# Even lag product ahead of the eight matches: two operations of an attention loop change places on VectorE and on TensorE

## What is computed

```python
qf, kf = fft(q, axis=2), fft(k, axis=2)                 # over the 64 tokens of a sequence
corr = ifft(qf * conj(kf), axis=2).real                 # correlation at 64 lags
w, idx = top_k(corr.transpose(0, 1, 3, 2), 8)           # the 8 best lags of each feature
w = softmax(w, axis=-1)
out = sum(w[i] * take(v, min(idx[i] + pos, 63)) for i in range(8))
x = x + out                                             # then x = x + moe(layernorm(x))
```

## Time and profile before

| | us |
|---|---|
| Median of 3 runs | 490.2 (487.67 to 490.48) |
| Profiled execution, whole time | 490.35 |
| Profiled execution, span of the core | 488.5 |
| Busy in the span: PE / DVE / ACT / POOL | 449.0 / 309.7 / 265.4 / 278.1 |
| Attention loop, from the first correlation maxima (pass 0) to those of pass 15 | 15.37 to 179.94 |
| One steady pass | 11.07 |

### The profile page before, as it was taken

The page is one execution under the profiler, slowest core; times in us unless marked ns, Lnnn a source line. Parts: engine busy times, 40 slices in busy tenths (PEclk is TensorE's granted clock), DMA queues, the critical chain, the costliest instruction groups (busy, mean ns, idle before and its releaser), DMA issues.

```text
span 488.5 us, 8388 instructions
## 1 busy us (share of the span) xinstructions
PE 449.0 (92%) x2272; PEld 334.6 (68%) x2272; DVE 309.7 (63%) x943; ACT 265.4 (54%) x521; POOL 278.1 (57%) x331
## 2 busy tenths in 40 slices
PE   3589999999999999958999998998999999999997
PEld 1456666655666664523368897897888999888885
DVE  2789899999999985488422647542333444248873
ACT  3868888888888873641102346554555665322120
POOL 2346667667666644494777287777656600077730
PEclk9989999999999999979999999998999999999999
DMA  4516733444443222211996568686888654268952
GB/s 160 194 43 235 283 130 129 150 165 160 162 144 130 86 88 86 84 46 57 316 388 251 208 221 304 239 303 223 290 261 291 204 198 152 108 176 259 320 194 86
DMA packets 40012, 91.89 MB, mean 188 GB/s; under 512 B 5024, under 2 KB 5024, under 8 KB 39712
## 3 DMA queue, kind: packets, MB, share of 16 engines
q1 hardware_dynamic: 32544, 62.00, 35.9%
q0 software_dynamic: 7424, 29.37, 17.8%
HBM read 49.92 MB, written 41.42 MB: 187 GB/s over the span
## 4 chain that ended last, share of the span: by engine, by line
PE 53%; DVE 16%; DMA 10%; issue 7%; POOL 7%; ACT 5%; SPq 1%; DVEq 0%; POOLq 0%; ACTq 0%
PE bank L471 36%; DMA x2T<-x_slots 7%; PE bank L656 4%; PE bank L572 3%; DVE top_v L955 3%; POOL arena L1215 3%; POOL arena L1218 3%; PE bank L483 3%; PE bank L581 3%; DMA resid<-x 2%; DVE stats L918 2%; DVE arena L960 2%; DVE resid L943 2%; ACT arena L787 1%; ACT arena L786 1%
## 5 line engine op out<-in xcount | busy, mean ns | idle before, releaser
L471 PE MATMUL bank<-ring,xgT_hi 128*128 x376 | 70.4, 285 | 0.0
L471 PEld LDWEIGHTS bank<-ring,xgT_hi 128*128 128x128 f32 x376 | 62.2, 193 | 4.0
L471 PE MATMUL bank<-ring,xgT_lo 128*128 x188 | 53.6, 285 | 0.0
L1103 DVE TENSOR_TENSOR xgT_lo<-bank,xgT_hi 128x512 fp32r<-128x512 f32 x47 | 32.3, 690 | 31.1 <-ACT xgT_hi L839 26.7
L1255 POOL TENSOR_TENSOR ring<-x2T,ring 128x1536 fp32r<-128x1536 f32 x14 | 49.3, 3520 | 1.2
L1303 POOL DMA_INDIRECT x2T<-y_rows,pos_i x16 | 16.2, 1014 | 43.1 <-DMA y_rows<-xg_sb 38.5
L1126 DVE TENSOR_TENSOR act_both<-bank,silu_sb 128x128 f32<-128x128 f32 x47 | 13.6, 290 | 41.2 <-ACT silu_sb L844 41.1
L733 ACT ACTIVATE silu_sb<-bank 128x512 f32<-128x512 f32 x16 | 9.6, 599 | 53.1 <-PE bank L471 36.9
L471 PE MATMUL bank<-tokens_hi,shgu_hi 128*128 128x512 f32 x96 | 37.8, 393 | 0.0
L1282 POOL CAST ring<-x2T 128x1536 fp32r<-128x1536 f32 x14 | 20.5, 1466 | 30.0 <-PE bank L471 29.6
L471 PE MATMUL bank<-tokens_hi,shgu_lo 128*128 128x512 f32 x96 | 37.4, 389 | 0.0
(11 more groups left out here) (159 smaller groups left out, 1241.3 us busy)
## 6 DMA issues: line engine op xcount, KB each, us to landing
x2T<-w_experts POOLq DMA_DIRECT2D x16, 768.0 KB, 5.5
x_slots<-x2T SPq DMA_DIRECT2D x47, 256.0 KB, 2.6
x2T<-x_slots SPq DMA_DIRECT2D x47, 256.0 KB, 3.0
y_rows<-xg_sb SPq DMA_DIRECT2D x47, 256.0 KB, 3.0
resid<-x SPq DMA_DIRECT2D x16, 256.0 KB, 3.3
arena<-ctx SPq DMA_DIRECT2D x16, 256.0 KB, 3.5
x_rows<-arena SPq DMA_DIRECT2D x16, 256.0 KB, 2.0
result<-resid SPq DMA_DIRECT2D x16, 256.0 KB, 3.9
```

Source lines behind the costliest of these rows:

```text
L471: last = mm(ps, a[i], b[k], start=start and n == 0, stop=stop and n == len(terms) - 1)
L1103: tt(dst, src, hi.bitcast(F32), ALU.subtract).then_inc(done, 1)
```

## The change

Two things change places, and one wait names another semaphore. TensorE makes the even lag product first and the odd one second; the wait for the logits stays with the even product and so comes ahead of both. VectorE does the two multiplications of the even lag spectrum (pair n-1) ahead of the eight matches (pair n), and their wait for the even product comes ahead of the matches with them. ScalarE's copy L764 waits for the odd product of the pass before, as that is now the last to read `lagwT`. The counts of instructions are the same on all engines.

```diff
@@ TensorE
                     pe.wait_ge(lagwT_ready, p + 1)
-                    mm(ps_w_odd[:, :], C["odd"], lagwT, start=True, stop=True).then_inc(w_odd_psum, 1)
                     wait(pe, logits_ready, p - 1)
                     mm(ps_w_even[:, :], C["even"], lagwT, start=True, stop=True).then_inc(w_even_psum, 1)
+                    mm(ps_w_odd[:, :], C["odd"], lagwT, start=True, stop=True).then_inc(w_odd_psum, 1)
@@ ScalarE
                     act.wait_ge(lagwT_psum, p + 1)
-                    wait(act, w_even_psum, p)
+                    wait(act, w_odd_psum, p)
                     copy(lagwT, ps_T[:, :]).then_inc(lagwT_ready, 1)
@@ VectorE
                     tt(segs(expz), lags, largest.to_broadcast([P, SEGS, L]), ALU.subtract).then_inc(centered, 1)
+                if live(n, -1):
+                    p, pb = pair(h, b, -1)
+                    dve.wait_ge(w_even_psum, p + 1)
+                    tt(out_prod[0], ps_w_even[:, :], ctx_even[pb], ALU.mult)
+                    tt(out_prod[1], ps_w_even[:, :], ctx_even_sw[pb], ALU.mult).then_inc(out_products_ready, 1)
+                if live(n, 0):
+                    p, _ = pair(h, b, 0)
+                    lags, tops = segs(ps_corr[:, :]), segs(top_v[:, :])
                     wait(dve, lagwT_psum, p)
                     apart(dve, dve_passed)
                     for s in range(SEGS):
                         last = nc.vector.match_replace(segs(lagw)[:, s], tops[:, s], lags[:, s], TAKEN)
                     last.then_inc(lags_marked, 1)
-                if live(n, -1):
-                    p, pb = pair(h, b, -1)
-                    dve.wait_ge(w_even_psum, p + 1)
-                    tt(out_prod[0], ps_w_even[:, :], ctx_even[pb], ALU.mult)
-                    tt(out_prod[1], ps_w_even[:, :], ctx_even_sw[pb], ALU.mult).then_inc(out_products_ready, 1)
```

## The result

The changed kernel took 500.28 us (median of 4 runs, 497.37 to 502.53), the kernel before 489.87 in the same comparison (4 runs, 487.67 to 490.48): a ratio of 1.0218, with a 95% interval from 1.0149 to 1.0286. It is slower, by about the forecast amount (499.5, range 494.6 to 502.5).

What follows compares the result with a forecast made beforehand. It took a ring through POOL, PE and DVE (L943 to L985), with a second side through L1215 holding L978, as the bound. 7.8 + 0.3 + 0.1 + 0.95 = 9.15 on 490.35 gave 499.5 us, range 494.6 to 502.5.

Steps and rivals of the forecast that it cites:

- Even product on DVE: Behind L960, DVE stands still for the even product until 105.02 instead of starting at 104.35: 0.67 us.
- Odd product on ACT: The odd product comes second, so L786 starts at 105.87, not 105.27, and L1215 runs 0.60 us later.
- Where both meet: At masked multiplication L978, held by L1215, both delays join: it ends 0.60 us later, paid again each pass.
- the reading that I took: L978 ends a fixed time behind L1215: 0.60 us a pass, 7.8 over thirteen passes.
- the quoted rule: Skill page: a two-SBUF-input VectorE instruction and a GpSimd SBUF read take turns, the second blocked; it gives 0.60 a pass.
- the other reading: L978 takes 1.10 us from its own slot: 0.67 a pass, 8.7 over thirteen passes.
- The count of passes: Loop sum: thirteen passes at 0.60, pass 1 at 0.3, pass 4 at 0.1, pass 16 at 0.95 us.
- Behind the loop: After the last logits nothing takes the delay up; the rest moves along as a whole, its length unchanged.
- Hidden but for a little: L978 not held in its new place, DVE alone sets the pass: 0.25 a pass, 494.6; chance 0.12 with no effect.
- Faster: L978 free of L1215 and even product there when L960 is done: 0.32 a pass shorter, 485.5 us; chance 0.06.
- Dearer: Waits add up, L978 stretched by a whole 1.10 behind the latest slot: 0.86 a pass, 504.2 us; chance 0.06.
- the signs that I had named: DVE idle about 0.6 before the even multiplication, L786 released by the odd product, L978 near 1.1, pass 11.67.

Runs made afterwards that it cites:

- the three kernels without it: Masked multiplication reads its second operand in PSUM, in the changed kernel, the kernel before and that with TensorE's half: 11.39, 10.69 and 11.05 us a pass.
- VectorE's half alone: The changed kernel with TensorE's order of before, odd lag product first: 504.32 us against 487.78, ratio 1.0350, 12.10 a pass.
- TensorE's half: The kernel before with only TensorE's products swapped, even lag product first, VectorE's list unchanged: 494.46 us against 487.78, ratio 1.0147.

## Why the prediction was right

*Even product on DVE: 0.67 forecast, 0.72 in the trace.* From the end of POOL's sum the first even multiplication starts 5.76 later (103.06 to 108.82), and the slot behind L960, 0.60 behind that operation's start, would have been 5.04 later: 0.72. The small miss is the start of the product: I took 0.05 behind the copy, as behind L764, and it was 0.14 behind L772 (107.55 to 107.69). Without the wait for the logits it was 0.05 again (104.96 to 105.01 in the kernel with the logits in another bank). The page of the profile counts 8402 instructions, 14 more than before, and 14 passes have that wait beside the one for the lag weights; with the logits in another bank two passes have it, and the page of that profile counts 8390. An instruction for the second wait fits the 0.09, but what it costs by itself was not tried.

*Odd product on ACT: 0.60 forecast, 0.66 in the trace.* L786 starts 6.62 behind the sum's end, and before 5.96. It carries the same 0.06 or so.

*Where both meet: 0.60 a pass forecast, 0.67 measured.* The step held in its mechanism. L981 started within POOL's product and ended 0.56 behind it, forecast 0.54; the two are the same within the rounding of the rows. What was too small is the delay that reaches this place, by the 0.06 of the product's start. That the second SBUF operand is what lets POOL hold it is shown by the three kernels without it, and a fixed length is ruled out by VectorE's half alone, so the reading that I took, and that the quoted rule makes, was the right one of the two. That the pass came out at the 0.67 of the other reading is a coincidence.

*The count of passes.* Passes 5 to 15 brought 6.63 (10 x 0.60 = 6.0 forecast). Passes 0 to 4 brought 1.07, where I had 0.3 + 0.60 + 0.60 + 0.1 = 1.6 for passes 1 to 4. Pass 2 brought 0.52 and not 0.60: no logits are copied yet in passes 1 and 2, so the even product waits for L764 alone there, and the 0.52 is near the 0.54 of a pass with the logits in another bank. My sum had charged that wait from the start. Passes 3 and 4 brought 0.32 and 0.38, together the 0.70 forecast, though not as 0.60 and 0.1. Passes 0 and 1 together were 0.17 shorter than before, where I had 0.3 longer; pass 0 took 7.05 before and 8.60 after, though nothing is changed in it, and pass 0 takes from 7.05 to 9.57 in the kernels of this study, so I leave the cause of that part open. Pass 15 and pass 16 brought 1.70 (0.60 + 0.95 = 1.55 forecast); L786 of pass 16 went from 192.35 to 202.76, and its copies, not POOL's roots, now release the normalisation. The first 0.69 of the table lie ahead of the first instruction that was changed, and are none of it. Without them the loop is 9.4 longer, forecast 9.15. That the sum is so close owes something to luck: 0.63 too little in the steady passes and 0.5 too much in the first ones nearly cancel.

*Behind the loop: as long as before, forecast.* From the router's first maximum to the end it was 283.6 us before and 285.7 after. Kernels of this study that are the same behind the loop and compute the same took 281.7 to 285.7 there: 282.6 with TensorE's half, 284.6 with VectorE's, 282.0 with the odd multiplication first. So 2.1 lies within what executions differ by, and I count none of it as the change's. This scatter is larger than the 0.8 us between the forecast and the median, so the lengths of the passes are the better test of the forecast.

*The rivals.* "Hidden but for a little" needed a masked multiplication that is free: it was held, and even without the hold the pass was 0.32 above that of the kernel before, where I had 0.25. "Faster" fell with the idle bracket of 0.64 ahead of the even multiplication. "Dearer" needed the stretch to be added whole; VectorE's half alone shows that it goes as soon as POOL is done. Of the signs that I had named, the brackets at L964 and at L786, the end of L981 and the pass (11.67 forecast, 11.74) are all there, and the normalisation of pass 16 comes 10.1 later (193.88 to 203.97; 9 forecast), of which 0.69 are not the change's.

One sentence ahead of the prediction was not exact: the lists of the engines' operations have the same counts, but the profile counts those 14 more instructions, as said; all of them are semaphore instructions on TensorE.

## What to carry to other kernels

Before an operation is moved ahead of work that covers its input, compare when that input lands with when its new slot opens: here the matches had covered about 0.7 us in which the product was still being made. Look for every chain that ends at the same point, since a change that delays two chains by the same amount is charged once, and undoing one half of it may cost more than leaving both. And if a sum on another engine waits for an operation that stands behind a slow one without needing it, try to move that operation first; here the move, which also freed the masked multiplication of its hold, was worth 0.9% without any new instruction.

## What the runs showed of the hardware

I had not expected that the order at the shared access between DVE and POOL could flip from pass to pass. In the kernel with TensorE's half alone L1215 starts ahead of L978 in every pass from 5 to 14. In four of these L978 starts 0.066 to 0.069 us behind it, and POOL's product was the one held (1.89 us); in the other six it starts 0.071 to 0.112 behind, and DVE's operation was held (1.72 to 1.77). So the order turns at 0.07 us and not at 0 in this run. Whether the start that the trace shows for POOL lies ahead of the moment that decides, or that for DVE behind it, no run tells. The Trainium skill, page "SBUF — State Buffer", section "SBUF: two separate sides", says that whichever starts first gets the access for the whole instruction; the lengths here agree (a held operation ends a little less than its own length behind the other one: 0.55 in 119.08 + 1.74 against 118.98 + 1.29, where it takes 0.69 alone, and 1.13 in 107.80 + 1.89 against 107.87 + 0.69, where it takes 1.29), but the trace's start times decide the order only when they lie further apart than a tenth of a microsecond or so.
